# A wider side block and another order of work in a linear layer with per-sample low-rank terms

## What is computed

```python
base = x @ W_base.T + b_base                  # x 2048 x 1024, W 1024 x 1024
a = x @ A.T                                   # A 16 x 1024
Bu, Bi = B_user[user_indices], B_item[item_indices]   # 1250 x 1024 x 16 each
user_part = einsum('bor,br->bo', Bu, a)
item_part = einsum('bor,br->bo', Bi, a)
common_part = a @ W_common.T
return base + 2.0 * (user_part + item_part + common_part)
```

## Time and profile before

| | |
|---|---|
| median of 3 runs | 216.55 us (216.5 to 216.77) |
| profiled execution | 216.55 us, of it a span of 214.5 us |
| TensorE busy | 209.8 us, 98% |
| VectorE busy | 165.0 us, 77% |
| GpSimd busy | 73.6 us, 34% |
| ScalarE busy | 59.1 us, 28% |
| mean granted clock of TensorE | 0.998 |

### The profile page before, as it was taken

The page is one execution under the profiler, slowest core; times in us unless marked ns, Lnnn a source line. Parts: engine busy times, 40 slices in busy tenths (PEclk is TensorE's granted clock), DMA queues, the critical chain, the costliest instruction groups (busy, mean ns, idle before and its releaser), DMA issues.

```text
span 214.5 us, 3020 instructions
## 1 busy us (share of the span) xinstructions
PE 209.8 (98%) x1112; PEld 175.3 (82%) x1112; DVE 165.0 (77%) x244; ACT 59.1 (28%) x97; POOL 73.6 (34%) x82
## 2 busy tenths in 40 slices
PE   7999999999999999999999999999999999999993
PEld 7777888797878889788887888878887888888782
DVE  1899799499999699799999889499966997063411
ACT  3788546526010521231103041073102400000000
POOL 8010550021626322145642475115552310374300
PEclk9999999999999999999999999999999999999999
DMA  6999999496489967798899889956989891347571
GB/s 202 391 409 407 282 419 383 128 282 252 133 272 310 383 252 278 260 312 309 267 270 352 343 296 295 344 227 206 335 244 393 339 327 78 113 150 174 154 148 49
DMA packets 14671, 57.75 MB, mean 269 GB/s; under 512 B 3812, under 2 KB 4196, under 8 KB 10668
## 3 DMA queue, kind: packets, MB, share of 16 engines
q0 software_dynamic: 7344, 35.30, 49.8%
q1 hardware_dynamic: 7024, 21.73, 27.8%
q10 hardware_dynamic: 288, 0.52, 0.7%
HBM read 58.95 MB, written 11.01 MB: 326 GB/s over the span
## 4 chain that ended last, share of the span: by engine, by line
PE 98%; DVE 0%; issue 0%; POOL 0%; POOLq 0%
PE main_ps L1090 23%; PE main_ps L1091 23%; PE main_ps L1092 23%; PE main_ps L1148 4%; PE main_ps L1121 4%; PE ps_a L1031 3%; PE main_ps L1125 3%; PE main_ps L1129 3%; PE ps_a L1030 3%; PE main_ps L1006 2%; PE main_ps L1141 2%; PE ps_a L1071 1%; PE ps_b L1042 1%; PE ps_a L1034 0%; PE ps_a L1072 0%; PE ps_b L1061 0%
## 5 line engine op out<-in xcount | busy, mean ns | idle before, releaser
L768 DVE SCALAR_TENSOR_TENSOR acc<-rows,a_entry,acc 128x1024 f32<-128x1024 f32 x75 | 96.2, 1283 | 7.4 <-DMA rows<-table,fetch 5.3
L409 POOL DMA_INDIRECT rows<-table,fetch x40 | 54.9, 1373 | 98.9 <-DVE acc L768 85.6
L1090 PE MATMUL main_ps<-w_hi,x_hi 128*128 128x512 f32 (+1 forms) x224 | 86.9, 388 | 0.0
L1091 PE MATMUL main_ps<-w_lo,x_hi 128*128 128x512 f32 (+1 forms) x224 | 85.9, 384 | 0.0
L1092 PE MATMUL main_ps<-w_hi,x_lo 128*128 128x512 f32 (+1 forms) x224 | 85.6, 382 | 0.0
L1090 PEld LDWEIGHTS main_ps<-w_hi,x_hi 128*128 128x128 f32 x224 | 42.1, 188 | 7.2
L1092 PEld LDWEIGHTS main_ps<-w_hi,x_lo 128*128 128x128 f32 x224 | 42.0, 188 | 7.1
L1091 PEld LDWEIGHTS main_ps<-w_lo,x_hi 128*128 128x128 f32 x224 | 42.1, 188 | 6.9
L547 ACT ACTIVATE out_sb<-main_ps 128x976 f32<-128x976 f32 (+1 forms) x12 | 11.9, 992 | 37.2 <-PE main_ps L1092 36.4
L667 DVE TENSOR_TENSOR x_lo<-x_lo_raw,x_hi 128x1024 fp32r<-128x1024 f32 (+2 forms) x19 | 19.9, 1052 | 0.2
L493 ACT ACTIVATE x_hi<-x_lo_raw 128x1024 fp32r<-128x1024 f32 (+2 forms) x18 | 16.8, 945 | 4.1 <-DMA x_lo_raw<-x_t 4.1
(11 more groups left out here) (115 smaller groups left out, 161.3 us busy)
## 6 DMA issues: line engine op xcount, KB each, us to landing
out<-out_sb SPq DMA_DIRECT2D x15, 512.0 KB, 5.1
x_lo_raw<-x_t SPq DMA_DIRECT2D x14, 512.0 KB, 8.4
w_lo_raw<-w_t SPq DMA_DIRECT2D x7, 512.0 KB, 7.2
x_lo_raw<-x_t SPq DMA_DIRECT2D x3, 256.0 KB, 5.5
rows<-table,fetch POOLq DMA_INDIRECT x40, 8.8
w_lo_raw<-w_t ACTq DMA_DIRECT2D x2, 256.0 KB, 4.0
set_sums<-acc SPq DMA_DIRECT2D x1, 512.0 KB, 2.6
out<-out_sb SPq DMA_DIRECT2D x2, 256.0 KB, 2.0
```

Of the source, the lines that this page charges most:

```text
L409: pool.indirect_dma_start(out=rows[:, n % SLOTS, :], out_offset=None, in_=table_chunks, in_offset=bass.IndirectOffsetOnAxis(ap=fetch[:, s, ...
L768: return dve.scalar_tensor_tensor(to, rows_r, a_r, to, ALU.mult, ALU.add)
L1090: pe.matmul(to, x_hi[:, u % RING, k, x], w_hi[:, k, o], start=start, stop=False)
L1091: pe.matmul(to, x_hi[:, u % RING, k, x], w_lo[:, k, o], start=False, stop=False)
```

## The change

`SIDE` goes from 48 to 112 columns, so that A's 16 and W's last 112 are a full block of 128. There is no `a_w` any more: A's 16 columns stand behind W's 1024 in `w_hi` and `w_lo` (`WIDE_F` = 1040), and `rank_a` takes columns 912 to 1039 of both, in three matmuls of 256 columns for each k, for all units, the first too. `first_tiles` and `base_step` have 400 columns in their second part, for tiles 0 and 1 too, and these get an `add_side` as well. `rank_a` waits until all of W has its low part. `take_turned` is two copies. `low` and `left`, the sources of `turn_low`, have two buffers. The orders on all engines are changed up to unit 1, and `first_tiles(7)` leaves out its product with `w_lo`, which `finish_first` does at the end of tiles 0 and 1. SP's order is as it was.

```diff
-SIDE = (P - 2 * R) // 2
+SIDE = P - R
 MAIN_F = OUT_F - SIDE
-BESIDE = R + SIDE
+WIDE_F = OUT_F + R
+SIDE_RING = 4
-TURNS_A = ("at0", "at1", "lt0", "at2", "lt1", "at3", "lt2", "lt3", "at4", "lt4", "at5", "lt5", "at6", "lt6", "at7",
+TURNS_A = ("at0", "at1", "at2", "lt0", "lt1", "at3", "lt2", "lt3", "at4", "lt4", "at5", "lt5", "at6", "lt6", "at7",
...
 def sides_before(n):
-    return min(n, FIRST_BACK) - UT
+    return min(n, FIRST_BACK)
...
             def store(t):
                 sp.wait_ge(evacuated, t + 1)
-                if UT <= t < FIRST_BACK:
+                if t < FIRST_BACK:
                     sp.wait_ge(side_added, sides_before(t + 1))
...
-            pool.memset(a_w[:, :, :, R:BESIDE].bitcast(f32), 0.0).then_inc(side_cleared, 1)
...
-            def put_side():
...
-                c = OUT_F if n < UT else MAIN_F
-                act.activation(out_sb[:, n % 2, 0:c], main_ps[n % MAINS][:, 0:c], ACT.Copy).then_inc(evacuated, 1)
+                act.activation(out_sb[:, n % 2, 0:MAIN_F], main_ps[n % MAINS][:, 0:MAIN_F], ACT.Copy).then_inc(evacuated, 1)
...
             make_w_hi(7)
-            copy_at(0)
             act.wait_ge(last_loaded, 16 * BLOCKS)
...
-            put_side()
+            copy_at(0)
+            make_x_hi(3, 0)
+            make_x_hi(3, 1)
             first_part(0)
+            copy_at(1)
             second_part(0)
             spread_a(0)
-            copy_at(1)
-            make_x_hi(3, 0)
-            copy_low(0)
             first_part(1)
-            make_x_hi(3, 1)
             second_part(1)
             spread_a(1)
             copy_at(2)
+            copy_low(0)
+            first_part(2)
+            second_part(2)
+            spread_a(2)
             act.wait_ge(shared_lo, 2)
             evacuate(0)
-            first_part(2)
-            second_part(2)
             evacuate(1)
             copy_low(1)
-            spread_a(2)
             copy_at(3)
             copy_low(2)
             make_x_hi(4, 0)
...
-                dve.tensor_reduce(a_side[:, UT * u:UT * (u + 1), :],
-                                  turned_ps.rearrange("p (t h r) -> p t r h", t=UT, h=2),
-                                  axis=AX.X, op=ALU.add).then_inc(bank_b_taken, 1)
+                dve.tensor_copy(side[:, u % SIDE_RING, :, :], turned_ps[:, :, 0:SIDE])
+                dve.tensor_copy(a_all[:, UT * u:UT * (u + 1), :], turned_ps[:, :, SIDE:P]).then_inc(bank_b_taken, 1)
...
             make_w_lo(3)
+            make_x_lo(0, 3)
+            make_w_lo(4)
...
+            make_x_lo(0, 4)
+            dve.wait_ge(a_hi_done, 1)
+            o = slice(OUT_F, WIDE_F)
+            dve.scalar_tensor_tensor(w_lo[:, :, o], a_raw[:, :, :], 2.0, w_hi[:, :, o].bitcast(f32),
+                                     ALU.mult, ALU.subtract).then_inc(a_lo_done, 1)
...
             dve.wait_ge(bank_b_taken, turn_b("rank") + 1)
+            make_w_lo(5)
             make_onehot(0)
-            make_x_lo(0, 3)
-            make_w_lo(4)
-            make_x_lo(0, 4)
...
-            make_w_lo(5)
-            take_rows(0)
             make_w_lo(6)
             make_x_lo(1, 0)
+            take_rows(0)
+            make_x_lo(1, 1)
             make_w_lo(7)
-            make_x_lo(1, 1)
...
-            take_turned(0)
             make_x_lo(2, 0)
-            spread_values(0)
...
             make_x_lo(2, 1)
             make_onehot(1)
+            take_turned(0)
+            make_x_lo(3, 0)
+            spread_values(0)
+            make_x_lo(3, 1)
             take_turned(1)
-            make_x_lo(3, 0)
             spread_values(1)
-            make_x_lo(3, 1)
             take_turned(2)
             spread_values(2)
             take_rows(1)
             take_entries(0)
-            row_products(0, range(0, 2))
+            row_products(0, range(0, 1))
+            add_side(0)
+            row_products(0, range(1, 2))
+            add_side(1)
             make_onehot(2)
             take_a(3)
...
             def rank_a(u):
                 wait_x_lo(u)
-                if u:
-                    pe.wait_ge(side_ready, 2)
+                pe.wait_ge(w_lo_done, KC + 1)
                 my_bank_a(f"at{u}")
-                both = a_w.rearrange("p k h r -> p k (h r)")
+                o = slice(MAIN_F, WIDE_F)
                 for k in range(KC):
-                    if k:
-                        pe.matmul(at_ps[0:BESIDE, :], a_w[:, k, 0, :], x_lo[:, u % RING, k, :], start=False, stop=False)
-                    done = pe.matmul(at_ps, both[:, k, :], x_hi[:, u % RING, k, :], start=(k == 0),
-                                     stop=(k == KC - 1))
-                    if k == 0:
-                        pe.matmul(at_ps[0:BESIDE, :], a_w[:, k, 0, :], x_lo[:, u % RING, k, :], start=False, stop=False)
+                    pe.matmul(at_ps, w_hi[:, k, o], x_hi[:, u % RING, k, :], start=(k == 0), stop=False)
+                    pe.matmul(at_ps, w_lo[:, k, o], x_hi[:, u % RING, k, :], start=False, stop=False)
+                    done = pe.matmul(at_ps, w_hi[:, k, o], x_lo[:, u % RING, k, :], start=False, stop=(k == KC - 1))
...
             def wait_main(t):
                 if t >= MAINS:
                     pe.wait_ge(evacuated, t - MAINS + 1)
-                    if UT <= t - MAINS < FIRST_BACK:
+                    if t - MAINS < FIRST_BACK:
                         pe.wait_ge(side_added, sides_before(t - MAINS + 1))
...
+            def finish_first(t):
...
+                k, x = KC - 1, slice(t * P, (t + 1) * P)
+                for half in range(HALVES):
+                    o = columns_of(half)
+                    done = pe.matmul(main_ps[t][:, o], x_hi[:, 0, k, x], w_lo[:, k, o], start=False, stop=True)
+                return done
...
-            for k in range(3):
+            for k in range(5):
                 first_tiles(k)
             rank_samples()
-            first_tiles(3)
-            first_tiles(4)
+            first_tiles(5)
+            first_tiles(6)
             pack_rows(0)
-            first_tiles(5)
+            base(2, range(0, 1), start=True)
+            first_tiles(7)
             pe.wait_ge(a_lo_done, 1)
-            pe.wait_ge(side_cleared, 1)
             rank_a(0)
-            first_tiles(6)
+            base(2, range(1, 2))
             turn_at(0)
-            first_tiles(7)
             rank_a(1)
-            base(2, range(0, 1), start=True)
+            base(2, range(2, 3))
             turn_at(1)
+            rank_a(2)
+            base(2, range(3, 4))
+            turn_at(2)
             turn_low(0)
-            base(2, range(1, 2))
-            rank_a(2)
+            base(2, range(4, 5))
+            pack_rows(1)
             left_of(0, (False, False))
-            last_of(0, stop=True).then_inc(tile_done, 1)
-            last_of(1, stop=True).then_inc(tile_done, 1)
-            turn_at(2)
-            base(2, range(2, 3))
-            pack_rows(1)
+            last_of(0)
+            last_of(1)
+            finish_first(0).then_inc(tile_done, 1)
+            finish_first(1).then_inc(tile_done, 1)
             turn_low(1)
-            base(2, range(3, 4))
             pack_entries(0)
-            base(2, range(4, 5))
+            base(2, range(5, 6))
             rank_a(3)
-            base(2, range(5, 6))
-            turn_low(2)
             base(2, range(6, 7))
             turn_at(3)
+            turn_low(2)
             left_of(1, (False, True))
```

More of the change, by code:

```diff
@@ L158, in rec_kernel @@
         x_raw, x_lo = two("x_lo", [P, RING, KC, US])
-        w_raw, w_lo = two("w_lo", [P, KC, OUT_F])
+        w_raw, w_lo = two("w_lo", [P, KC, WIDE_F])
         x_hi_raw, x_hi = two("x_hi", [P, RING, KC, US])
         acc = sb("acc", [P, ACCS, OUT_F])
-        w_hi = sb("w_hi", [P, KC, OUT_F], f32r)
+        w_hi = sb("w_hi", [P, KC, WIDE_F], f32r)
         sums = [acc[:, i, :] for i in ACC_OF]
@@ L500, in make_w_hi @@
                 act.wait_ge(w_loaded[k], 16)
[L501 removed]
+                act.activation(w_hi[:, k, 0:OUT_F], w_raw[:, k, 0:OUT_F], ACT.Copy).then_inc(w_hi_done, 1)
             def first_part(u):
@@ L566, in _ @@
             act.wait_ge(a_loaded, 16)
-            act.activation(a_w[:, :, 0, 0:R], a_raw[:, :, :], ACT.Copy, scale=2.0).then_inc(a_hi_done, 1)
+            act.activation(w_hi[:, :, OUT_F:WIDE_F], a_raw[:, :, :], ACT.Copy, scale=2.0).then_inc(a_hi_done, 1)
             make_w_hi(3)
@@ L677, in make_w_lo @@
                 dve.wait_ge(w_hi_done, k + 2)
-                dve.tensor_tensor(w_lo[:, k, :], w_raw[:, k, :], w_hi[:, k, :].bitcast(f32),
+                c = slice(0, OUT_F)
+                dve.tensor_tensor(w_lo[:, k, c], w_raw[:, k, c], w_hi[:, k, c].bitcast(f32),
                                   ALU.subtract).then_inc(w_lo_done, 1)
@@ L790, in sum_brought @@
                 beside = brought_sums[of[0]][:, MAIN_F:OUT_F]
-                link(dve.tensor_tensor(beside, beside, a_side[:, t, R:BESIDE], ALU.add))
```

(24 more changed lines are left out.)

58 lines of the change are left out of this document (27 added, 31 removed).

## The result

The changed kernel takes 219.99 us (median of 4 runs, 219.55 to 220.72), the kernel before 216.65 us beside it: a ratio of 1.0158, with a 95% interval of 1.0123 to 1.0193. It is slower by 3.3 us, where 1.0 us slower was forecast and the range ended at 219.5. The profiled execution took 220.41 us, with a span of 218.8. A run more than 1.5% above the fastest of its kernel counts as slow and stands in no ratio; there was one in experiment 1 and one in experiment 2, both named there.

A forecast was written before the change was run, and what follows sets the result against it. TensorE was taken to bound the kernel, busy 209.8 of 214.5 us. Unit 2 late by 4.3, then -7.7 + 3.7 + 0.6, and 0.1 for evacuations, gave +1.0 us: 217.6 us, range 214.9 to 219.5.

The forecast's parts named there:

- Columns: TensorE's second-part matmuls shrink to 400 columns: 9.0 us less over 14 tiles, 2.2 us less for tiles 0 and 1.
- `rank_a`: TensorE's low-rank block: 24 matmuls in place of 16, at 117 ns each, 7.5 us more over eight units.
- The rule of the Trainium skill: Weight loads overlap a running matmul only in another row group; by it `rank_a` adds 13.6 us (rival 229 us, chance 0.03).
- Waits while W arrives: New TensorE waits at k = 1, k = 5, `rank_a(0)` and `rank_a(3)`: together 1.6 us (1.0 to 2.1).
- holding back k = 7 wins nothing: Ahead of `rank_a(0)`: it needs all eight `w_lo`, so delaying the last third of k = 7 gains nothing.
- The wait that is late next: x for unit 4, queued behind `store(0)`, delays `add_side(2)`: TensorE waits 1.9 us and starts unit 2 some 4.3 us late.
- the 0.6 us at `pack_entries(1)`: Late `take_a(3)` on VectorE also makes TensorE wait some 0.6 us at `pack_entries(1)`, before unit 2.
- TensorE to its end: From unit 2 to the end: 4.3 - 7.7 + 3.7 + 0.6 = +0.9, and 0.1 for wider evacuations: +1.0 us.
- The sum of work alone: TensorE's matmul work without waits: -9.0 - 2.2 + 7.5 = -3.7 us; as a rival 212.8 us, chance 0.05.
- The tail: Program's end: VectorE's end stays TensorE's, as it idled 4.29 us before its last sum; TensorE's +1.0 us gives 217.6.
- the prediction's own signs of being wrong: In the trace after: unit 2 starts less than 3 us late, or `rank_a` takes over 3 us.

The follow-up runs named there:

- experiment 1: On the changed kernel, GpSimd adds set 2 to the output before it brings the fifth set back, not after: 217.85 us, ratio 1.0036.
- experiment 2: On the changed kernel, the two loads of x for unit 4 go ahead of the store of tile 0 in SyncE's queue: 217.81 us, ratio 1.0021.
- Experiments 5: On the kernel of experiment 3, VectorE makes the low part of W's step 5 ahead of the ranks, not behind them: 215.15 us, ratio 0.9917.
- experiment 7: Experiment 5's kernel, with `copy_low(1)` between the first two evacuations and `make_x_lo(6, 1)` one chunk of products earlier: 214.07 us, ratio 0.9876.
- experiment 6: On the kernel of experiment 3, the product with W's low part is held back for k = 6, not k = 7: 215.69 us, ratio 0.9946.
- experiment 3: The changed kernel with the edits of experiments 1 and 2 together: 215.7 us, ratio 0.9934; again in the second batch, 215.88 us, 0.995.

## Why the prediction was right, and where it failed

**Columns: right.** The same 21 starts as in the earlier trace rows, now with 400 columns:

```profile
207.58 0.34 PE L1082 MATMUL main_ps<-w_hi,x_hi 128*128 128x400 f32 x1
...
211.40 0.35 PE L1082 MATMUL main_ps<-w_hi,x_hi 128*128 128x400 f32 x1
```

3.82 us for 21 matmuls, 182 ns each, where 183 was the sum's. Over a whole unit, from the beginning of unit 6 to that of unit 7, TensorE took 22.71 us before and takes 21.47: 48 matmuls give 25.8 ns each, where 26.7 was taken, and 0.62 us a tile, where 0.64 was taken. For tiles 0 and 1 the sum had 47 ns a matmul, where its own 227 and 183 ns differ by 44; a k went from 2.73 us to 2.47, where 2.45 was taken.

**`rank_a`: right, but for a restart.** Its first call begins at 27.84 and tile 2 goes on at 30.76: 24 matmuls in 2.92 us with the restart, where the sum took 24 x 117 ns = 2.81. The first four calls take 2.91 to 2.94 us, the one of unit 4 takes 2.83. A load of 128 columns every 118 ns is no bound here, as the earlier trace rows had it. The rule of the Trainium skill that the prediction weighed ("TensorE: Matmul & The Clock Gate", section "The mechanism") does not hold in this trace.

**Waits while W arrives: right in place and in sum, 1.5 us where 1.6 was said.** By the view of waits: 0.5 us at k = 1 (0.28 said), 0.6 at k = 5 (0.8), 0.2 at `rank_a(3)` (0.3); the one ahead of `rank_a(0)` is 0.2 by the starts around it (0.2). Experiments 5 and 7 took the second and the third away. That holding back k = 7 wins nothing is borne out by experiment 6 as far as an exchange with k = 6 can show it.

**The wait that is late next: right in mechanism, and in size by some luck.** Asked for at 49.0 (48.4 said), landed by 54.9 (55.0), `take_a(3)` over at 56.9 (57.2), `add_side(2)` through at 66.8 (67.1), a wait of 1.68 us (1.9), unit 2 4.08 us late (4.3). Experiment 2 shows the cause to be the load's place behind the store, for it moves nothing else. But pairs of misses cancel in it. The loads were asked for 0.6 us later than forecast, and the first landed in 5.9 us and not 6.6: with a store and a gather beside it, it took 0.2 us more than the 5.7 of the earlier trace rows without a gather. TensorE would have been at unit 2 at 66.91 - 1.68 = 65.23, where 65.2 was said, though the 0.6 us at `pack_entries(1)` did not come; against that, the first four calls of `rank_a` took 0.4 us more than was taken for them.

**TensorE to its end: right.** The last sum is 1.15 us late where 1.0 was forecast. The sum of work alone can be read from experiment 7, where nearly all waits are gone: 216.9 - 214.07 = 2.8 us were won, with 0.3 us of waiting left, where the sum said 3.7. The restarts and the 0.02 us a tile make up most of the difference.

**The tail: this step failed.** The prediction put it so: "VectorE's end stays TensorE's: it idled 4.29 us before its last sum", and turned TensorE's lateness straight into the program's. It looked at two of the engines that end the program and left out the third, GpSimd, which puts the cost of its lateness at nothing. GpSimd's last additions stand behind `bring_back`, which stands behind VectorE's last product, and VectorE was late by more than TensorE's end: 186.62 against 181.93, 4.7 us. VectorE waits for TensorE at the last `take_a`, and is 5.0 us late there; first the kernel before, then the one after:

```profile
139.12 0.43 DVE L718 TENSOR_REDUCE a_side<-ps_b 128x128 f32<-128x256 f32 x1 [3.17 <-PE ps_b L1042]
```

```profile
144.08 0.39 DVE L706 COPY side<-ps_b 128x224 f32<-128x224 f32 x1 [3.93 <-PE ps_b L1031]
```

Behind it VectorE has the same products to do as before and wins next to nothing back (42.5 us to their end, 42.8 before), while TensorE has no more `rank_a` and wins back 0.62 us with each tile. From there each step of the chain added: the first gather 5.3 us late, the addition of set 2 5.6, that of set 3 6.3, its landing 8.5, and GpSimd's `DRAIN` 8.5. The slack was 4.2 us, from the end of that `DRAIN` at 210.1 to SyncE's at 214.3. So the span ends 6.6 us behind the last sum, where it ended 3.5 behind it in the kernel before and in experiment 1. None of the prediction's own signs of being wrong (unit 2 less than 3 us late, `rank_a` over 3 us) could show this. Whoever writes down an end has to carry each engine's own lateness to it, against that engine's own slack.

Of the excess of 3.3 us the tail is some 2.6 (ratio 1.0158 to 1.0036 in experiment 1), and the rest is TensorE's lateness, as forecast. Not settled: why the last addition took 8.6 us to land and not 6.4, and why SyncE waited 3.8 us behind its last store and not 1.7 as before. Both fall together in the kernel after, where the addition and the last two stores are under way at once; no run here takes that apart.

## What to carry to other kernels

When an engine that bounds the kernel is given less work, carry the lateness of every other engine to the end of the program too: what lay hidden under the bound with a few microseconds of slack ends it as soon as one engine falls behind by more than that. A store made to wait holds up all that is queued behind it on the same issuing queue, and what it delays (here a load, then a copy, then the products) can come back as a wait of the engine that bounds the kernel (1.7 us here); loads that need nothing from the store belong ahead of it (here they went out at 45.0 and not at 49.0). And price a change's orders apart from its idea: here the wider block was worth having (214.07 us with the orders mended, and the kernel before had no wait of TensorE behind the start that an order could have won), while the orders that came with it cost more than it won.

## What the runs showed that was not expected

The time scatters more after the change. The kernel before took 216.5 to 216.8 us in the four runs beside the kernel after, and within 1.0 us over 25 runs of the first batch; the kernel after goes from 219.55 to 220.72 in four, and experiment 2's from 215.85 to 219.27 in twelve. Where the addition of set 2 is moved and TensorE sets the end again, the runs of experiments 5 and 7 lie within 0.6 and 0.8 us (214.77 to 215.37, 213.6 to 214.43).

Two runs with the same edit do not fit: 220.84 us in experiment 1, which has no trace, and 217.46 in experiment 3, which has one. In that one GpSimd's `DRAIN` ends at 208.6 in a span of 215.8, so it is not the tail. TensorE waits at `rank_a(7)` for the low part of x, because VectorE, which makes it, had waited 2.7 us for gathered table rows between 120 and 131, where it waited 1.2 in the second trace of the same kernel:

```profile
138.25 0.39 PE L1025 MATMUL ps_a<-x_hi,w_hi 128*128 128x256 f32 x1 [1.28 <-DVE x_lo L658]
```

The other traces of the changed kernels have no such wait there. So the scatter has more than one place. How much the additions at the end give to it is not shown: each kernel has one trace, experiment 3's two.
